# Experts stage: a store and a broadcast change places on SyncE, three steps move one unit, and an fp32 bias product becomes one fp16 product

## The chip, the cores and the metric

The kernel runs on one core of a Trainium2 chip. The metric is the device time of one execution in microseconds, as the median of several runs.

## The reference

The input is 4096 tokens of 128 channels (8 batches of 512, or 4 of 1024, as the layers see them). Six residual steps follow one another, each on a normalised copy of x:

```python
x = x + 0.5 * L0_ffn(layernorm(x))     # gate, up, down with a hidden width of 384
x = x + L0_attn(layernorm(x))          # time mixing with a scan over the tokens
x = x + 0.5 * L0_ffn(layernorm(x))
x = x + 0.5 * L1_ffn(layernorm(x))     # experts
x = x + L1_attn(layernorm(x))          # flow attention, causal
x = x + 0.5 * L1_ffn(layernorm(x))     # experts, the same weights
```

The change touches the experts step, cut to what matters:

```python
xn = (x - mu) * rsqrt(var + EPS) * ln_gamma + ln_beta
abel_out = gelu(xn @ abel_w + abel_b)
logits = xn @ moe_gate_w + moe_gate_b                        # 8 experts
topw, topi = top_k(logits, 2)
w_dense = sum(one_hot(topi, 8) * softmax(topw)[..., None])   # 8 weights a token, 2 of them not 0
h = gelu(einsum('bsd,edh->ebsh', xn, ew1) + eb1)             # 8 experts of width 256
eo = einsum('ebsh,ehd->ebsd', h, ew2) + eb2                  # eb2: the bias of the second layer, [8, 128]
moe_out = einsum('ebsd,bse->bsd', eo, w_dense)               # so eb2 comes in as w_dense @ eb2
moe_out = moe_out @ expm(gens[0]) @ expm(gens[1]) @ expm(gens[2])
gate = sigmoid(concatenate([abel_out, moe_out]) @ gc_w + gc_b)
mixed = abel_out * (1 - gate) + moe_out * gate
return residual + mixed
```

## The kernel before

x stays in SBUF for the whole program (`X`). Each of the six steps is a stage, and each stage runs over 8 chunks of 512 tokens. The stages and the order of every engine's work are written out by hand: each engine has a function per stage with a `step(i, p, lead, mid, lag)` that is called once per chunk. `mid` is the work on chunk i, `lead` prepares chunk i+1, `lag` finishes chunk i-1; the first call has only `lead`, the last only `lag`. Engines meet at semaphores. An instruction waits until its semaphore's count is reached, and everything behind it on its engine waits with it.

In the experts stages (numbers 4 and 6) the `mid` work on a chunk has 16 units u, two halves of 128 rows of each expert. Matrix products with fp32 accuracy are made of three fp16 products, high by high, high by low and low by high (`three`, lines 1474 to 1478). For each unit:

- TensorE makes the first layer's product into one of five PSUM banks (three products, 128x512),
- ScalarE takes the gelu in the bank (line 993),
- VectorE multiplies with the token's weight for that expert, giving `hw` (line 1317); the weights must lie in all 128 partitions, in `mo.wB`,
- ScalarE copies `hw` to fp16 (`high`, line 989), one unit behind its gelu,
- GpSimd subtracts that copy from `hw` and keeps the rest as fp16 (`low`, line 786),
- TensorE adds the second layer's product (`second`, line 1643) into bank 5, six units later (SKEW); units 10 to 15 of it fall into the next chunk's units 0 to 3.

The second layer's weights have the three rotations and a factor WS = 64 folded in, and so has the bias: `ebw` holds the folded bias in its first 8 rows and zeros below, and one fp32 product of `ebw` with `mo.wT` opens the sum in bank 5 (line 1641, just before unit 0 of `second`). `mo.wT` holds the 8 weights of each token in its first 8 rows, zeros below (written by the memset of line 741).

Between these units lies the routing of chunk i+1 (`lead`): TensorE turns the normalised tokens (line 1559, unit 1), ScalarE copies them to fp32 and fp16 (lines 999 and 1000, unit 2), TensorE makes the logits (line 1670, unit 3), VectorE finds the two largest and their weights in short dependent steps (lines 1349 to 1371, units 4, 6 and 7), TensorE turns the result to 8 rows (line 1682, unit 9), and VectorE copies that into `mo.wT` (line 1382, unit 9). The bank of the logits and of the turned weights is also that of the abel product (unit 11), which therefore waits for the copy. The finishing of chunk i-1 (`lag`) is on VectorE lines 1310 (unit 3), 1323 (unit 5), 1341 and 1344 (unit 10) and 1203 (unit 13), on ScalarE the tanh of line 1005 (unit 9), on TensorE lines 1665 and 1677 (units 8 and 12). ScalarE also normalises chunk i+2, one tile each in units 10, 11, 12 and 15 (line 903).

SyncE carries the weights to all partitions: `routes(c)` waits for `mo.wT`, writes its 8 rows to DRAM (line 613), waits for that, and issues four broadcasts of two experts each (line 617). In the second experts stage it also stores the finished chunks: for each c it first does `routes` of the next chunk, then waits for x of chunk c and stores it (line 627). x of chunk c is finished in unit 13 of the step of chunk c+1 (line 1203); the weights of chunk c+2 are ready in unit 9 of that same step.

## Time and profile before

| | us |
|---|---|
| timed runs, median (lowest to highest of 3) | 1024.81 (1024.4 to 1026.99) |
| the profiled execution | 1027.39 |
| its span, first to last instruction | 1025.7 |
| TensorE busy | 859.0 (84%) |
| VectorE busy | 725.1 (71%) |
| ScalarE busy | 648.1 (63%) |
| GpSimd busy | 604.2 (59%) |
| first experts stage, from its first transposes to its last x (about) | 307 to 543 |
| second experts stage (about) | 775 to 1023 |

Times in the trace are microseconds from the start of the span. PE is TensorE, PEld its weight loads, DVE VectorE, ACT ScalarE, POOL GpSimd, SPq the DMA queue of SyncE. L1317 is line 1317 of the kernel. Behind an instruction, brackets give how long its engine had been idle and which instruction ended the wait. The busy time of TensorE counts a product to its modelled end; one product of 128x512 is 0.38 long, and the next starts earlier.

### The profile page before, as it was taken

What the parts mean: (1) busy time and instruction counts of PE and PEld (TensorE: products, weight loads), DVE (VectorE), ACT (ScalarE), POOL (GpSimd) and SP (SyncE); (2) the same over time, 40 slices, a digit from 0 to 9 for tenths busy, and PEclk for the clock granted to TensorE, in tenths of its full rate; (3) what the DMA queues carried; (4) which work ended last, traced back from release to release, by engine and by line L of the source; (5) the groups of instructions that cost most, each with busy time, mean ns of one, the idle gap of its engine ahead of it and who ended that gap; (6) DMA issues with size and microseconds to landing.
All of it is one profiled execution on the core that took longest, in us unless ns stands there. A gap on an engine that the chain in (4) does not pass through costs nothing.

```text
span 1025.7 us, 14084 instructions
## 1 busy us (share of the span) xinstructions
PE 859.0 (84%) x3830; PEld 459.1 (45%) x3830; DVE 725.1 (71%) x1549; ACT 648.1 (63%) x1169; POOL 604.2 (59%) x611
## 2 busy tenths in 40 slices
PE   7889777678966999999994888888866998889997
PEld 6744333373423444444442455555534444444443
DVE  6945479964555788888872477777784878877774
ACT  3177499957745888888763343333324878777874
POOL 2164776566468776666673354444457757555664
PEclk9989799969986999999997899999986999999999
DMA  8000000000002222222200000000002221122220
GB/s 209 11 2 0 0 1 1 0 1 2 0 0 83 83 84 83 82 83 82 82 1 1 0 1 1 1 1 1 1 0 83 84 73 46 68 93 93 93 93 21
DMA packets 27406, 42.10 MB, mean 41 GB/s; under 512 B 5320, under 2 KB 19036, under 8 KB 27356
## 3 DMA queue, kind: packets, MB, share of 16 engines
q1 hardware_dynamic: 27356, 41.52, 12.2%
q8 instruction: 21, 0.34, 0.2%
q14 instruction: 29, 0.24, 0.1%
HBM read 39.15 MB, written 2.36 MB: 40 GB/s over the span
## 4 chain that ended last, share of the span: by engine, by line
PE 28%; issue 26%; POOL 21%; DVE 16%; ACT 5%; DMA 1%; SPq 1%; POOLq 1%; DVEq 0%; ACTq 0%
POOL arena L786 10%; PE bank L1476 5%; PE bank L1478 5%; PE bank L1477 5%; POOL arena L806 5%; POOL arena L750 4%; PE bank L1700 3%; DVE arena L1317 1%; ACT bank L993 1%; DVE stats L1166 1%; PE bank L1670 1%; PE bank L1707 1%; PE bank L1559 1%; DMA arena<-wrows 1%; ACT arena L989 1%
## 5 line engine op out<-in xcount | busy, mean ns | idle before, releaser
L786 POOL TENSOR_TENSOR arena<-arena 128x512 f16<-128x512 f32 x256 | 294.5, 1162 | 141.7 <-ACT arena L989 139.9
L1317 DVE TENSOR_TENSOR arena<-bank,arena 128x512 f32<-128x512 f32 x256 | 173.6, 685 | 89.7 <-ACT bank L993 48.5
L989 ACT ACTIVATE arena<-arena 128x512 f16<-128x512 f32 x256 | 161.3, 630 | 81.5 <-DVE arena L1317 81.0
L993 ACT ACTIVATE bank<-bank,eb 128x512 f32<-128x512 f32 x256 | 167.1, 657 | 18.1 <-PE bank L1478 17.2
L1477 PE MATMUL bank<-arena,ew1hi 128*128 128x512 f16 x256 | 101.6, 397 | 0.0
L813 POOL TENSOR_TENSOR arena<-arena 128x512 f32<-128x512 f32 (+1 forms) x24 | 32.7, 1372 | 117.0 <-DVE arena L1440 89.8
L1476 PE MATMUL bank<-arena,ew1hi 128*128 128x512 f16 x256 | 101.2, 395 | 0.0
L1478 PE MATMUL bank<-arena,ew1lo 128*128 128x512 f16 x256 | 101.1, 395 | 0.0
L1476 PE MATMUL bank<-arena,ew2hi 128*128 128x512 f16 x256 | 97.1, 379 | 0.8 <-POOL arena L786 0.6
L1477 PE MATMUL bank<-arena,ew2hi 128*128 128x512 f16 x256 | 97.0, 379 | 0.0
L1478 PE MATMUL bank<-arena,ew2lo 128*128 128x512 f16 x256 | 97.0, 379 | 0.0
L750 POOL TENSOR_TENSOR arena<-arena 128x512 f16<-128x512 f32 x48 | 54.8, 1157 | 58.0 <-ACT arena L917 58.0
L1707 PE MATMUL bank<-arena,until 128*128 128x512 f32 x128 | 63.2, 617 | 14.3 <-DVE arena L1396 13.1
L1476 PE MATMUL bank<-arena,f0hi 128*128 128x512 f16 x144 | 57.4, 399 | 16.7 <-POOL arena L750 13.5
L806 POOL TENSOR_TENSOR arena<-arena 128x1024 f32<-128x1024 f32 x32 | 61.7, 1949 | 0.0
L1407 DVE SCALAR_TENSOR_TENSOR arena<-arena,bank 128x1024 f32<-128x1024 f32 x16 | 19.5, 1222 | 54.4 <-PE bank L1700 54.4
L1477 PE MATMUL bank<-arena,f0hi 128*128 128x512 f16 x144 | 57.3, 398 | 0.0
L1478 PE MATMUL bank<-arena,f0lo 128*128 128x512 f16 x144 | 56.9, 395 | 0.0
L1227 DVE SCALAR_TENSOR_TENSOR arena<-bank,arena 128x512 f32<-128x512 f32 x48 | 33.0, 691 | 33.8 <-ACT arena L924 29.5
L903 ACT ACTIVATE Z<-X,nbias,rstd 128x128 f32<-128x128 f32 (+1 forms) x128 | 52.5, 487 | 5.4 <-POOL pool_spare L723 5.4
L1559 PE MATMUL bank<-ident,Z 128*128 128x128 f32 x192 | 31.9, 292 | 26.4 <-ACT Z L903 14.0
L1335 DVE TENSOR_SCALAR X<-X,keep,shift (+1 forms) x64 | 52.1, 818 | 0.0
(273 smaller groups left out, 1879.5 us busy)
## 6 DMA issues: line engine op xcount, KB each, us to landing
arena<-wrows SPq DMA_DIRECT2D x64, 512.0 KB, 5.6
X<-in_L_attn_x_dram SPq DMA_DIRECT2D x8, 256.0 KB, 4.3
out_dram<-X SPq DMA_DIRECT2D x8, 256.0 KB, 2.3
arena<-in_L_ffn_ew_dram SPq DMA_DIRECT2D x2, 512.0 KB, 6.5
arena<-in_L_ffn_ew_dram SPq DMA_DIRECT2D x1, 1024.0 KB
wrows<-arena SPq DMA_DIRECT2D x16, 16.0 KB
arena<-in_L_ffn_gens_dram SPq DMA_DIRECT2D x1, 192.0 KB, 2.6
arena<-in_L_ffn_w_gate_dram SPq DMA_DIRECT2D x1, 192.0 KB, 2.8
```

The lines of the kernel that those rows point to most:

```text
L750: pool.tensor_tensor(f0.hlo[:, u, :], f0.h[:, u % 2, :], f0.hhi[:, u, :], ALU.subtract).then_inc(S.hlo, 1)
L786: pool.tensor_tensor(mo.hlo[:, u % 8, :], mo.hw[:, u % 4, :], mo.hhi[:, u % 8, :], ALU.subtract).then_inc(S.hlo, 1)
L806: pool.tensor_tensor(fl.kv[:, b, :].rearrange("p (h m d) -> p h m d", d=HD, m=HD), key.to_broadcast([P, HEADS, HD, HD]), value.to_broadcas ...
L903: last = A(Z[:, zp, t * P:(t + 1) * P], X[:, bass.ds(tile * P, P)], ACT.Identity, bias=bias[:, bass.ds(tile, 1)], scale=scale[:, bass.ds(t ...
L989: A(mo.hhi[:, u % 8, :], mo.hw[:, u % 4, :], ACT.Copy).then_inc(S.hhi, 1)
L993: A(bank[MM1_BANK[u]][:, :], bank[MM1_BANK[u]][:, :], ACT.Gelu, scale=1.0 / WS, bias=eb1[:, u:u + 1]).then_inc(S.gelu, 1)
L1317: TT(mo.hw[:, u % 4, :], bank[MM1_BANK[u]][:, :], mo.wB[:, p, u // EB, :], ALU.mult)\
L1335: last = TS(tile, tile, keep[:, c], shift[:, c], ALU.mult, ALU.add)
L1476: mm(dst, whi, xhi, start=start, stop=False, skip_group_check=True)
L1477: mm(dst, whi, xlo, start=False, stop=False, skip_group_check=True)
L1478: return mm(dst, wlo, xhi, start=False, stop=stop, skip_group_check=True)
L1707: mm(bank[5 + h], until[:, :], fl.kv[:, b, h * CH:(h + 1) * CH], start=True, stop=True)\
```

## The change

Four edits, all in the experts stages or what prepares them:

1. SyncE stores chunk c-1 after the routing of chunk c+1 is sent, where it stored chunk c. The last store comes alone at the end.
2. The bias product becomes one fp16 product. `ebs` has the high part of the folded bias in rows 0 to 7 and 32 to 39 and its low part in rows 64 to 71; `mo.ws` has the high part of the weights in rows 0 to 7 and 64 to 71 and their low part in rows 32 to 39; all other rows are zero. ScalarE makes the two high parts of a chunk's weights from `mo.wT` in unit 15 of the chunk before (ahead of its last tile of normalising), VectorE the low part in unit 1 of the chunk itself, between line 1317 of units 0 and 1. The preparation of `ebs` takes three copies on ScalarE, where there was one, and a subtraction on VectorE in the third stage. The memset is of `mo.ws`, at the head of the third stage.
3. The turning of the routing weights and their copy move from unit 9 to unit 10, the abel product from unit 11 to unit 12.
4. In the first chunk of each experts stage ScalarE copies the next chunk's turned tokens after the gelu of unit 1, ahead of the fp16 copy of unit 0, where that was after unit 2's.

```diff
         ablo = sb("ablo", [P, P], F16)
-        ebw = sb("ebw", [P, P])
+        ebs = sb("ebs", [P, P], F16)
         gamma = sb("gamma", [P, 1])
...
         mo.wd = a.take([TILES, E])
-        a.used = max(a.used, TM_WORDS)
-        mo.wT = a.take([2, CH])
...
         fl.bdm = a.take([2, CH])
+        a.used = max(a.used, TM_WORDS)
+        mo.wT = a.take([2, CH])
+        mo.ws = a.take([2, CH], F16)
...
         MO.wd = sem("moe_wd")
+        MO.whi = sem("moe_whi")
+        MO.wlo = sem("moe_wlo")
         MO.wB = [sem(f"moe_wB{k}") for k in range(E // 2)]
...
         CREDIT = 1
+        Q = P // 4
...
             eng.wait_ge(FF.x, 2 * NCH + CREDIT)
-            eng.wait_ge(S0.flo, NU // TILES + 1)
+            eng.wait_ge(S0.flo, NU // TILES + 2)
             eng.wait_ge(S0.fhi, NU // TILES + 1)
...
+            def store(c):
+
+                sp.wait_ge(MO.x, c + (NCH + 1 + CREDIT))
+                sp.dma_start(out_parts[:, :, c:c + 1, :], X4[:, :, c:c + 1, :]).then_inc(stored, 16)
+
...
                     routes(NCH + c + 1)
-                sp.wait_ge(MO.x, c + (NCH + 1 + CREDIT))
-                sp.dma_start(out_parts[:, :, c:c + 1, :], X4[:, :, c:c + 1, :]).then_inc(stored, 16)
+                if c:
+                    store(c - 1)
+            store(NCH - 1)
             sp.wait_ge(stored, 16 * NCH)
...
                 pool.memset(blockones[:, :], 1.0).then_inc(S0.pool, 1)
-                pool.memset(ebw[:, :], 0.0).then_inc(S0.consts, 1)
+                pool.memset(ebs[:, :], 0.0).then_inc(S0.consts, 1)
                 pool.memset(ones[:, :], 1.0).then_inc(S0.consts, 1)
...
                     bias_parts()
-                    pool.memset(mo.wT, 0.0)
+                if number == 3:
+                    pool.wait_ge(S0.small2, 1)
+                    pool.memset(mo.ws, 0.0)
...
                 act.wait_ge(S0.consts, N_CONST)
-                A(ebw[0:E, :], bank[FOLD.small][0:E, P:2 * P], ACT.Copy, scale=WS).then_inc(S0.fhi, 1)
+                for row in (0, Q):
+                    A(ebs[row:row + E, :], bank[FOLD.small][0:E, P:2 * P], ACT.Copy, scale=WS)
+                A(sm.MT[0:E, :], bank[FOLD.small][0:E, P:2 * P], ACT.Copy, scale=WS).then_inc(S0.fhi, 1)
...
                         A(mo.hhi[:, u % 8, :], mo.hw[:, u % 4, :], ACT.Copy).then_inc(S.hhi, 1)
+                    def copies(i):
+                        act.wait_ge(S.tr, i + 2)
+                        A(mo.xn, bank[6][:, :], ACT.Copy).then_inc(S.xn, 1)
+                        A(mo.xhi[:, 1 - p, :], bank[6][:, :], ACT.Copy).then_inc(S.xhi, 1)
                     for u in range(NU):
...
                               bias=eb1[:, u:u + 1]).then_inc(S.gelu, 1)
+                            if u == 1 and not lag:
+                                copies(i)
                             if u:
                                 high(i, u - 1)
-                        if lead and u == 2:
-                            act.wait_ge(S.tr, i + 2)
-                            A(mo.xn, bank[6][:, :], ACT.Copy).then_inc(S.xn, 1)
-                            A(mo.xhi[:, 1 - p, :], bank[6][:, :], ACT.Copy).then_inc(S.xhi, 1)
+                        if lead and u == 2 and (lag or not mid):
+                            copies(i)
+                        if lead and u == NU - 1:
+                            act.wait_ge(S.wT, i + 2)
+                            for row in (0, 2 * Q):
+                                last = A(mo.ws[row:row + E, 1 - p, :], mo.wT[0:E, 1 - p, :], ACT.Copy)
+                            last.then_inc(S.whi, 1)
                         if onward and u in (10, 11, 12, 15):
...
                 TT(abel_b[:, :], abel_b[:, :], small[:, 2 * E + NU:2 * E + NU + 1], ALU.add).then_inc(S0.flo, 1)
+                dve.wait_ge(S0.fhi, NU // TILES + 1)
+                TT(ebs[2 * Q:2 * Q + E, :], sm.MT[0:E, :], ebs[0:E, :], ALU.subtract).then_inc(S0.flo, 1)
...
                     for u in range(NU):
+                        if mid and u == 1:
+                            dve.wait_ge(S.whi, i + 1)
+                            TT(mo.ws[Q:Q + E, p, :], mo.wT[0:E, p, :], mo.ws[0:E, p, :], ALU.subtract)\
+                                .then_inc(S.wlo, 1)
                         if lag and u == 3:
...
                                 add_to_x(i - 1, first, bank[6][:, :], 0.5, S.x, number)
-                        if lead and u == 9:
+                        if lead and u == 10:
                             dve.wait_ge(S.wpT, i + 2)
...
                             after(pe, S.dm, c)
-                            mm(bank[5][:, :], ebw[:, :], mo.wT[:, cp, :], start=True, stop=False,
+                            pe.wait_ge(S.wlo, c + 1)
+                            mm(bank[5][:, :], ebs[:, :], mo.ws[:, cp, :], start=True, stop=False,
                                skip_group_check=True)
...
                             pe.wait_ge(S.xn, i + 2)
+                            if mid:
+                                pe.wait_ge(S.wT, i + 1)
                             after(pe, S.abel, i)
...
                             last.then_inc(S.rT, 1)
-                        if lead and u == 9:
+                        if lead and u == 10:
                             pe.wait_ge(S.wpair, i + 2)
...
                             last.then_inc(S.wpT, 1)
-                        if mid and u == 11:
+                        if mid and u == 12:
                             if lead:
...
                             three(bank[7][:, :], abhi[:, :], ablo[:, :], mo.xhi[:, p, :], mo.xlo[:, p, :])\
```

## Rows read from the trace of the kernel before

**Rows 1.** busy by stretch: us, then PE, PEld, DVE, ACT, POOL; granted clock; DMA share, GB/s

```profile
433.20:460.40 27.20, 25.54 (x125) 12.50 (x125) 22.79 (x54) 22.68 (x44) 18.64 (x17) 1.00 0.22 78
876.70:907.10 30.40, 27.29 (x123) 12.94 (x123) 22.88 (x50) 22.42 (x43) 18.39 (x17) 0.94 0.24 78
```

**Rows 2.** timeline of TensorE (start us, us, instruction), the logits' products

```profile
351.80 0.95 PE L1670 MATMUL bank<-gate_g,arena 128*128 128x8 f32 x8
...
487.44 0.95 PE L1670 MATMUL bank<-gate_g,arena 128*128 128x8 f32 x8
...
818.08 0.95 PE L1670 MATMUL bank<-gate_g,arena 128*128 128x8 f32 x8
...
966.23 1.06 PE L1670 MATMUL bank<-gate_g,arena 128*128 128x8 f32 x8 [1.76 <-ACT arena L999]
```

**Rows 3.** timeline of TensorE, one middle chunk of the first experts stage

```profile
435.99 1.02 PE L1641 MATMUL bank<-arena,ebw 128*128 128x512 f32 x2
436.85 0.38 PE L1476 MATMUL bank<-arena,ew2hi 128*128 128x512 f16 x1
437.07 0.38 PE L1477 MATMUL bank<-arena,ew2hi 128*128 128x512 f16 x1
...
444.17 0.60 PE L1682 MATMUL bank<-ident,arena 128*8 128x128 f32 x4 [1.66 <-DVE arena L1371]
```

**Rows 4.** timeline of ScalarE, the same chunk

```profile
432.27 0.59 ACT L999 ACTIVATE arena<-bank 128x512 f32<-128x512 f32 x1
...
446.02 0.66 ACT L993 ACTIVATE bank<-bank,eb 128x512 f32<-128x512 f32 x1
...
454.56 0.63 ACT L989 ACTIVATE arena<-arena 128x512 f16<-128x512 f32 x1
```

**Rows 5.** timeline, the copy and the logits: first stage, then second

```profile
433.03 1.08 PEld L1670 LDWEIGHTS bank<-gate_g,arena 128*128 128x128 f32 x8
...
846.84 0.59 ACT L999 ACTIVATE arena<-bank 128x512 f32<-128x512 f32 x1
...
847.48 1.06 PE L1670 MATMUL bank<-gate_g,arena 128*128 128x8 f32 x8 [2.10 <-ACT arena L999]
```

**Rows 6.** waits of the second stage; timeline of SyncE's queue and VectorE

```profile
DVE arena L1317 <- DMA arena<-wrows: 25.5, 6, 4.4
...
837.57 0.39 SPq L627 DMA_DIRECT2D out_dram<-X  x1
...
840.03 1.81 SPq L617 DMA_DIRECT2D arena<-wrows  x4
...
844.41 1.29 DVE L1317 TENSOR_TENSOR arena<-bank,arena 128x512 f32<-128x512 f32 x2 [4.32 <-DMA arena<-wrows]
...
456.85 1.29 DVE L1317 TENSOR_TENSOR arena<-bank,arena 128x512 f32<-128x512 f32 x2 [1.47 <-ACT bank L993]
```

**Rows 7.** timeline of VectorE, the chunk of rows 3

```profile
446.29 0.67 DVE L1382 COPY arena<-bank 8x512 f32<-8x512 f32 x1
446.89 0.67 DVE L1317 TENSOR_TENSOR arena<-bank,arena 128x512 f32<-128x512 f32 x1
...
448.20 0.69 DVE L1344 SCALAR_TENSOR_TENSOR arena<-bank,arena 128x512 f32<-128x512 f32 x1
```

**Rows 8.** line 1364 (ns min/median/max), and GpSimd's timeline at the added subtraction

```profile
L1364 DVE TENSOR_TENSOR arena<-arena x16: 191/1030/1033, 313.1 to 974.7; 128x32 f32<-128x32 f32 x16
...
428.26 2.27 POOL L786 TENSOR_TENSOR arena<-arena 128x512 f16<-128x512 f32 x2 [0.84 <-ACT arena L989]
```

**Rows 9.** timeline, first chunk of the first stage, then of the second

```profile
325.74 5.61 POOL L786 TENSOR_TENSOR arena<-arena 128x512 f16<-128x512 f32 x5
...
328.28 0.69 DVE L1317 TENSOR_TENSOR arena<-bank,arena 128x512 f32<-128x512 f32 x1 [1.52 <-ACT bank L993]
...
790.39 1.88 PE L1670 MATMUL bank<-gate_g,arena 128*128 128x8 f32 x8 [4.01 <-ACT arena L999]
...
794.29 0.69 DVE L1317 TENSOR_TENSOR arena<-bank,arena 128x512 f32<-128x512 f32 x1 [1.59 <-ACT bank L993]
```

## The prediction, made before the changed kernel ran

> **What bounds the kernel now.** First the busy time by stretch [rows 1]: in a middle chunk of the first experts stage TensorE works 25.54 of 27.2 us at a granted clock of 1.00, ScalarE 22.68, VectorE 22.79. So TensorE leads, with little room behind it. Then the beat, from one chunk's gate logits (line 1670) to the next's [rows 2]. Five beats of the first experts stage take 487.44 - 351.80 = 135.64, 27.13 each. The same program in the second stage takes 966.23 - 818.08 = 148.15, 29.63 each. The question is what makes 27.13, and what adds 2.5 in the second stage.
>
> The timeline of one chunk answers the first. TensorE runs without a gap but for one: the transposes of the routing weights (line 1682) start at 444.17, after 1.66 us in which they wait for VectorE's line 1371 [rows 3]; with the 0.16 by which a product's modelled length (0.38) exceeds its step (0.22) the hole is 1.82. Then the chain on ScalarE: it copies the normalised input (line 999) at 432.27, and the logits' first weight load is at 433.03 [rows 4, 5]. Where TensorE did wait for that copy (846.84 to 847.48), it needed 0.64. So at 433.03 the copy had only 0.12 to spare; over the six like places I find 0 to 0.32 and take 0.18. ScalarE's chain (copy, logits, gelu, VectorE's routing chain, then gelus and fp16 copies without a gap to the next line 999) is thus 26.95 long against TensorE's 27.13: two loops of nearly one length. From the gelu at 446.02 to the copy at 454.56 ScalarE runs without a gap but the last 0.2: each operation starts some 0.52 after a copy of 0.63 and 0.57 after a gelu of 0.66 [rows 4].
>
> The waits answer the second [rows 6]: VectorE's line 1317 sat 25.5 us in six waits for the broadcast of the routing weights. SyncE issues the store of the previous chunk at 837.57 and the broadcasts only at 840.03; the first line 1317 that needs them starts at 844.41, after 4.32 of waiting. In the first stage, which stores nothing, the same instruction (456.85) waits 1.47, and for its gelu. SyncE held a finished routing row back for a store whose data came later. So the stall is 4.32 - 1.47, 2.85 a chunk, and ScalarE's loop there is 847.48 - 818.08 = 29.40 less 2.85, some 26.5 (shorter than in the first stage, for no statistics are taken there) [rows 2, 5].
>
> **The change part by part.**
>
> *SyncE.* The store of chunk c-1 now comes after the broadcasts of chunk c+1. All six stalls go: 2.85 each where ScalarE's loop is next. The weights are copied later (below), by 449.30 in the chunk of rows 3; even with the whole 2.46 from 837.57 to 840.03 after it, and the 4.38 from 840.03 to 844.41, line 1317 could start at 456.1, and it is wanted at 456.85 or later. The store now runs beside the last broadcasts, but their parts are used four or more units later.
>
> *TensorE's bias product.* fp32, 435.99 to 436.85, 0.86; as one fp16 product it is one step, 437.07 - 436.85 = 0.22 [rows 3]. It saves 0.64 a chunk, but ahead of the wait for line 1371, which VectorE and not TensorE sets: worth nothing in chunks with a successor, 0.64 in each last one.
>
> *Unit order.* The transposes move one unit on, behind six products (1.29). That fills 1.29 of the 1.82 hole. But VectorE's copy (line 1382), now in unit 10, stands behind hw, and in a middle chunk behind lines 1341 and 1344. It was at 446.29. hw of unit 10 can start when the gelu of 446.02 (0.66) is done, 446.71, so 0.18 before its 446.89; line 1344 then starts at 448.02, and the copy at 448.63 to 449.30 [rows 7]. TensorE, after its transposes (0.60 long, 0.44 by step) at 444.17 and four groups of three products, is at 447.2, waits for line 1344 to end (448.71), turns that result until 449.15, and waits for the copy until 449.36. With the abel product (three steps) behind it, unit 13's product comes at 450.01 instead of 449.58, so TensorE's loop is 27.13 + 0.43 = 27.56: the hole is not won but moved. The gelu of unit 13 lies in ScalarE's part without gaps, and TensorE is hardly ahead of it there: it starts some 0.42 later. ScalarE's loop takes that too, as does VectorE's, whose copy filled a slot that is now idle.
>
> *ScalarE's two added copies.* Of 8 x 512, at unit 15, in the part without gaps. No row shows such a copy on ScalarE. From below, nothing, if they fell into waits; from above 2 x 0.63 with no overlap. VectorE's copy of 8 x 512 takes 0.67, as much as its 128 x 512 ones at 0.67 to 0.69 [rows 7], so width and not partitions counts there; I take the step of ScalarE's 128 x 512 copies, 2 x 0.52 = 1.04. The Trainium skill (ScalarE: Activation LUTs, What ACT_TABLE_LOAD costs) speaks against the change here: an ACTIVATE goes by its elements per lane, 186 ns + 0.833 ns each, neighbours overlapping by 93 ns, whatever the partitions. By that page two cost an estimated 1.04 as well; if they went by all elements, they would be worth some 0.2.
>
> *VectorE's added subtraction* (8 x 512, between hw of unit 0 and of unit 1): 0.60 by its step. The fp16 copy of unit 1 follows a gelu and a copy later, so 0.02 of it shows. Its danger is GpSimd: line 1364 takes 0.19 to 1.03 us for the same 32 elements a partition [rows 8], the long ones beside a GpSimd operation. Here GpSimd's pair of low parts (428.26 to 430.53) ends near its place (430.44); with the fp16 copy of unit 15 moved as much as the gelu of unit 0, by some 1.46, I have the last one end 0.1 before the subtraction starts. The Trainium skill (GPSIMD Engine Reference, Specifications) says that VectorE instructions with two SBUF inputs contend with GpSimd for the SBUF interface; the long rows agree, and it is a rival below.
>
> *First chunk.* The copies of line 999 go ahead of the fp16 copy that waits for the broadcast. In the second stage the logits waited 4.01 for them (790.39), and hw of unit 4 was at 794.29 [rows 9]. Now its gelu can go right after those of units 2 and 3, and hw comes at 791.75: 2.5 earlier. In the first stage hw of unit 4 must wait until GpSimd has done its first low part, one of five from 325.74 (5.61, 1.12 each): 326.9 against 328.28, 1.4. At the end of these chunks the added copies take 1.04 back, less where ScalarE had been waiting (TensorE, not ScalarE, was late there); net 1.6 and 2.0 gained.
>
> *Rest.* The memset moves to the start of the third stage, GpSimd idle there before its first low part, under 1 us: nothing. Two more small copies at the end of mixing, at most 2 x 0.52: 0.3. One small subtraction in the third stage: nothing. New waits (whi, wlo, wT before the logits) find their work done half a chunk ago.
>
> *Sum.* First experts stage: beat 26.95 + 1.04 + 0.42 = 28.4, against 27.13 that is +1.2 to +1.3, five times +6.1; start -1.6; last chunk +0.43 - 0.64 = -0.2. Together +4.3. Second: beat 26.5 + 1.04 + 0.42 + 0.1 = 28.06, five of them 140.3 against 148.15, -7.8; start -2.0; into the last chunk and through it -1.6 (its stall is partly behind TensorE, 1.2; +0.43; -0.64; the rest of the tail 0.2). Together -11.4. With +0.3: -6.8. The profiled execution took 1027.39 (span 1025.7), so 1020.6; that one lies 2.6 above the median of the timed runs, 1024.81, from which it is 1018.0.
>
> **The rivals.**
> A. ScalarE's copies hide, and TensorE's loop of 27.56 binds. For it: ScalarE is busy only 22.68 of 27.2 [rows 1]. Against: its idle time is before units 5 to 7, in waits for VectorE, not at unit 15. Then the first stage gains 4.0 against my sum and the second 2.5: -13.3, 1011.5.
> B. The other sign: VectorE's subtraction is held by a GpSimd low part in each chunk. Place: between hw of units 0 and 1; price: up to 1.03 - 0.19 = 0.84 and what is left of the GpSimd operation (1.14), say 1.1 a beat, on ScalarE's loop, 12 beats, +13: 1031. It decides from 0.6 a beat on. For it, [rows 8]; against, the order of times above, and that only what exceeds 0.1 shows.
> C. TensorE's clock. The stretch at 876.70 has 0.94 of the full clock (products at the lower of the two levels, 1.2 GHz, after a pause before the logits) and is 30.40 long [rows 1]; the beat from 818.08, with such a pause and no fall, was 29.40. So 1.0 for each fall. My pauses (1.2 at line 1682, under 1 before the logits) are shorter than the present 1.82, which brings no fall. Seven of twelve beats would take the gain, twelve give 1030.
> D. The change doesn't do what it says: the broadcasts stay last, since the copy that feeds them moved back. Then the second stage keeps 29.6 a beat: 1018.0 + 7.8 = 1025.8.
>
> **How the numbers follow.** Forecast 0.60, A 0.20, B 0.08, C 0.06, D 0.06. What a measurement of this kernel can tell from no change is about 0.3%, 3.1 us. The forecast (its own range 1014 to 1022: copies 0.8 to 1.26, slack 0 to 0.32, copy's delay 0.2 to 0.6, each ten times) is faster nearly always, A always; B slower; C and D are the same or slower. Faster 0.79, same 0.12, slower 0.09. The range reaches into A below and near C above: 1010 to 1024.5.
>
> **What would show it.** In the trace after: no wait of line 1317 for the broadcast but the first of each stage; in both stages a beat of 28.1 to 28.4, the second stage gaining 1.5 a beat and the first losing 1.2; line 1682's hole shorter, a new one before the abel product; TensorE waiting for line 999 in every middle chunk, 0.5 to 0.9; two added copies of 0.6 each on ScalarE. The forecast is wrong if the first stage's beat stays at 27.1 to 27.6 (A), if the added subtraction is over 1.2 long (B), if clocks under 0.97 stand in middle chunks (C), or if waits for the broadcast remain (D).

## The result and the profile after

| | before | after |
|---|---|---|
| timed runs, median (lowest to highest, 13 each) | 1027.14 (1024.4 to 1030.39) | 1032.29 (1030.23 to 1034.93) |
| the profiled execution, its span | 1027.39, 1025.7 | 1031.05, 1029.3 |
| TensorE, VectorE, ScalarE, GpSimd busy | 859.0, 725.1, 648.1, 604.2 | 850.2, 735.4, 668.1, 606.8 |

The change makes the kernel slower by 0.50% (ratio 1.0050, 95% interval 1.0036 to 1.0065), some 5 us. The forecast was 1018.0. Of the 14.3 us between the two, 2.3 are the starting point: the forecast was counted from 1024.81, the median of three runs, where thirteen have 1027.14. As a difference, -6.8 was forecast and +5.1 measured. One of the executions behind the tables below (of "the same with the units of before") took 1276.51 us at a granted clock of 0.64, the four others of that version 1019.37 to 1021.56; it is left out.

The copy of the normalised input (line 999 before, line 1006 after) starts once a chunk and cuts the span into pieces. Timeline of ScalarE in the kernel before, the third and the eighth (last) such copy of each experts stage:

```profile
350.71 0.59 ACT L999 ACTIVATE arena<-bank 128x512 f32<-128x512 f32 x1
...
486.41 0.58 ACT L999 ACTIVATE arena<-bank 128x512 f32<-128x512 f32 x1
...
817.08 0.59 ACT L999 ACTIVATE arena<-bank 128x512 f32<-128x512 f32 x1
...
965.59 0.59 ACT L999 ACTIVATE arena<-bank 128x512 f32<-128x512 f32 x1
```

The same of the kernel after:

```profile
352.15 0.58 ACT L1006 ACTIVATE arena<-bank 128x512 f32<-128x512 f32 x1
...
497.08 0.58 ACT L1006 ACTIVATE arena<-bank 128x512 f32<-128x512 f32 x1
...
827.07 0.58 ACT L1006 ACTIVATE arena<-bank 128x512 f32<-128x512 f32 x1
...
970.14 0.58 ACT L1006 ACTIVATE arena<-bank 128x512 f32<-128x512 f32 x1
```

Five beats of the first stage take 144.93 after 135.70 (28.99 each, 27.14 before); of the second 143.07 after 148.51 (28.61 each, 29.70 before). With the first copy of each stage as a further cut, every kernel of this study falls into seven pieces. "First" is from the first to the third copy (the start of the pipeline and the step of chunk 0, in which the second copy lies), "seam" from the last copy of the first experts stage to the first of the second (the flow attention stage lies in it), "end" from the last copy to the end of the span:

| kernel | start | first | 5 beats | seam | first | 5 beats | end | span |
|---|---|---|---|---|---|---|---|---|
| before | 308.4 | 42.3 | 135.7 | 289.1 | 41.6 | 148.5 | 60.1 | 1025.7 |
| after | 308.6 | 43.6 | 144.9 | 288.6 | 41.4 | 143.1 | 59.2 | 1029.3 |
| forecast of after, against before | +0.3 | -1.6 | +6.1 | -0.2 | -2.0 | -7.8 | -1.6 | -6.8 |
| measured, against before | +0.2 | +1.3 | +9.2 | -0.5 | -0.2 | -5.4 | -0.9 | +3.6 |
| SyncE's order alone | 307.1 | 42.7 | 135.6 | 287.9 | 42.8 | 135.4 | 59.2 | 1010.7 |
| SyncE, units, first chunk | 310.7 | 41.6 | 137.4 | 291.2 | 39.1 | 137.4 | 60.7 | 1018.1 |
| bias product alone | 308.7 | 44.8 | 142.9 | 290.3 | 43.8 | 152.6 | 61.3 | 1044.4 |
| later units alone | 306.7 | 42.7 | 137.4 | 292.9 | 41.6 | 148.5 | 60.5 | 1030.3 |
| SyncE and first chunk | 308.6 | 41.5 | 135.6 | 289.1 | 42.0 | 135.4 | 59.2 | 1011.4 |
| subtraction late | 309.2 | 42.8 | 143.1 | 296.4 | 40.5 | 141.4 | 59.6 | 1033.0 |
| all late | 308.7 | 41.8 | 139.2 | 297.0 | 39.4 | 138.3 | 62.0 | 1026.4 |
| all late, old units | 309.1 | 41.7 | 136.6 | 291.8 | 42.4 | 136.4 | 60.9 | 1018.9 |
| subtraction in unit 9 | 308.4 | 43.3 | 153.0 | 292.9 | 41.2 | 151.2 | 64.8 | 1054.7 |
| third copy | 309.6 | 44.3 | 147.0 | 291.1 | 41.7 | 146.3 | 59.8 | 1039.7 |
| after, again | 308.8 | 43.3 | 144.1 | 290.5 | 41.0 | 143.1 | 59.1 | 1029.9 |
| all late, again | 309.2 | 41.8 | 138.3 | 296.7 | 39.2 | 138.3 | 62.0 | 1025.5 |

Of the 10.4 us by which the span missed its forecast (+3.6 against -6.8), 3.1 and 2.4 lie in the beats, 2.9 and 1.8 in the first chunks, 0.2 in the rest. Each row is one execution, and single pieces differ by chance: the starts lie between 306.7 and 310.7, though nothing that takes time in them was changed between most of these kernels.

The middle chunk of the kernel after, busy time by stretch (columns as in [rows 1]), once in each stage, against [rows 1]:

```profile
439.61:468.21 28.60, 25.68 (x122) 11.90 (x122) 22.88 (x56) 23.77 (x45) 18.70 (x16) 1.00 0.23 74
884.38:913.05 28.67, 25.66 (x122) 11.87 (x122) 22.78 (x52) 23.75 (x45) 18.70 (x16) 1.00 0.27 83
```

TensorE is no longer the engine with no room: 25.7 of 28.6 us against 25.54 of 27.2, at full clock, and it waits. The first of these stretches is the shortest of its stage's five; the others are 29.24, 29.22, 29.00 and 28.87, and VectorE is busy 0.8 to 0.9 longer in each. The same chunk in this execution and in the second one of the same kernel (the last experiment):

```profile
381.39:410.61 29.22, 25.80 (x122) 11.88 (x122) 23.79 (x57) 23.86 (x46) 18.53 (x16) 1.00 0.23 74
```

```profile
380.99:409.92 28.93, 25.80 (x122) 11.89 (x122) 22.94 (x57) 23.86 (x45) 18.71 (x16) 1.00 0.20 75
```

The difference is one instruction, line 1364, in which VectorE finishes a normalised tile of x. Timeline of VectorE and of GpSimd in the kernel after, a long and a short case:

```profile
428.80 1.26 DVE L1364 TENSOR_SCALAR X<-X,keep,shift  x1
...
457.81 0.33 DVE L1364 TENSOR_SCALAR X<-X,keep,shift  x1
```

```profile
428.76 1.22 POOL L798 TENSOR_TENSOR arena<-arena 128x512 f16<-128x512 f32 x1 [0.73 <-ACT arena L1003]
...
457.76 1.39 POOL L798 TENSOR_TENSOR arena<-arena 128x512 f16<-128x512 f32 x1 [0.72 <-ACT arena L1003]
```

Both start 0.04 to 0.05 after a GpSimd subtraction, and either outcome occurs. It was long in four of the five beats here and in one of five in the second execution. Compared chunk by chunk, a beat of the first stage is 0.28 to 0.29 longer with the long case, whichever execution has it; without it the five beats would average 28.76. In the second stage the last beat takes 28.50 with it and 28.51 without.

Timeline of TensorE in the chunk from 439.61, the instructions ahead of which it had been idle, and the bias product:

```profile
440.24 1.06 PE L1702 MATMUL bank<-gate_g,arena 128*128 128x8 f32 x8 [0.73 <-ACT arena L1006]
...
443.10 0.38 PE L1671 MATMUL bank<-arena,ebs 128*128 128x512 f16 x1
...
447.19 1.13 PE L1695 MATMUL bank<-arena,ones 128*128 128x512 f32 x2 [0.47 <-DVE arena L1352]
...
451.28 0.60 PE L1714 MATMUL bank<-ident,arena 128*8 128x128 f32 x4 [0.37 <-DVE arena L1400]
...
455.89 0.66 PE L1709 MATMUL bank<-ident,arena 128*128 128x128 f32 x4 [1.43 <-DVE arena L1373]
```

The first row is the verdict on who binds: the logits wait 0.73 for ScalarE, where in the first experts stage before the copy still had 0.12 to spare (433.03 in [rows 5]). The fourth and fifth are the moved hole: 0.37 where [rows 3] had 1.66, and 1.43 at a new place. ScalarE around unit 15 and around the next copy, the same kernel:

```profile
461.93 0.64 ACT L1003 ACTIVATE arena<-arena 128x512 f16<-128x512 f32 x1
462.47 1.25 ACT L1022 ACTIVATE arena<-arena 8x512 f16<-8x512 f32 x2
463.75 0.49 ACT L917 ACTIVATE Z<-X,nbias,rr 128x128 f32 x1
```

```profile
438.18 0.64 ACT L1011 ACTIVATE bank<-bank,eb 128x512 f32<-128x512 f32 x1
439.08 0.63 ACT L1003 ACTIVATE arena<-arena 128x512 f16<-128x512 f32 x1 [0.26 <-DVE arena L1346]
439.61 0.58 ACT L1006 ACTIVATE arena<-bank 128x512 f32<-128x512 f32 x1
440.09 0.59 ACT L1007 ACTIVATE arena<-bank 128x512 f16<-128x512 f32 x1
```

VectorE at the second of these places:

```profile
436.84 0.69 DVE L1346 TENSOR_TENSOR arena<-bank,arena 128x512 f32<-128x512 f32 x1 [2.76 <-ACT bank L1011]
437.56 0.68 DVE L1333 TENSOR_TENSOR arena<-arena 8x512 f16<-8x512 f32 x1
438.27 1.36 DVE L1346 TENSOR_TENSOR arena<-bank,arena 128x512 f32<-128x512 f32 x2
```

The two added copies take 462.47 to 463.75, 1.28, in a part of ScalarE's work without gaps. The subtraction takes 437.56 to 438.27, and hw behind it comes so late that the fp16 copy of 439.08 waits for it, a wait that [rows 4] do not have at their like place (432.27 follows its forerunners without one). From the gelu of 438.18 to the copy of the input at 439.61 are 1.43; in the kernel before the same two starts (431.18 and 432.27) are 1.09 apart. The difference, 0.34, is the subtraction's price on ScalarE's loop. The broadcasts are early, as meant. Waits of VectorE over the whole kernel after (columns: us, times, longest), where the second stage alone had 25.5 us in six waits [rows 6], and SyncE's queue in its second stage:

```profile
DVE arena L1346 <- DMA arena<-wrows: 4.9, 1, 4.9
```

```profile
872.56 0.28 SPq L617 DMA_DIRECT2D wrows<-arena  x1
...
874.04 1.74 SPq L621 DMA_DIRECT2D arena<-wrows  x4
...
876.11 0.39 SPq L627 DMA_DIRECT2D out_dram<-X  x1
```

The one wait left is that of the first chunk of the first stage; the store (line 627) stands behind the broadcasts.

### The profile page after: what moved, and what is told of

Read it like the earlier page. It is cut to its first block, busy times and chain, and to the rows that moved or that the text cites. A ratio compares the mean times of both kernels' runs of the same rounds, so it can differ in the third digit from the quotient of the medians.

```text
span 1029.3 us, 14102 instructions
## 1 busy us (share of the span) xinstructions
PE 850.2 (83%) x3805; PEld 447.3 (43%) x3814; DVE 735.4 (71%) x1566; ACT 668.1 (65%) x1203; POOL 606.8 (59%) x611
## 4 chain that ended last, share of the span: by engine, by line
POOL 30%; issue 23%; PE 21%; DVE 16%; ACT 8%; POOLq 1%; SPq 1%; DVEq 0%; DMA 0%; ACTq 0%
POOL arena L798 22%; PE bank L1732 9%; POOL arena L762 4%; PE bank L1739 3%; DVE arena L1436 2%; POOL rstd L720 1%; DVE arena L1346 1%; ACT bank L1011 1%; PE bank L1505 1%; DVE stats L1191 1%; PE bank L1507 1%; DVE arena L1438 1%; PE bank L1506 1%; ACT L1073 1%; ACT arena L1063 1%
## 5 line engine op out<-in xcount | busy, mean ns | idle before, releaser
L1346 DVE TENSOR_TENSOR arena<-bank,arena 128x512 f32<-128x512 f32 x256 | 174.1, 686 | 90.3 <-ACT bank L1011 76.6
L1505 PE MATMUL bank<-arena,ew1hi 128*128 128x512 f16 x256 | 98.3, 384 | 1.2 <-DVE arena L1346 1.2
L1506 PE MATMUL bank<-arena,ew1hi 128*128 128x512 f16 x256 | 98.3, 384 | 0.0
L1507 PE MATMUL bank<-arena,ew1lo 128*128 128x512 f16 x256 | 98.1, 383 | 0.0
L1425 DVE TENSOR_TENSOR arena<-bank,arena 128x512 f32<-128x512 f32 x64 | 42.4, 686 | 11.0 <-PE bank L1739 10.9
```

Of the source, the lines that this page charges most:

```text
L1346: TT(mo.hw[:, u % 4, :], bank[MM1_BANK[u]][:, :], mo.wB[:, p, u // EB, :], ALU.mult)\
L1505: mm(dst, whi, xhi, start=start, stop=False, skip_group_check=True)
L1506: mm(dst, whi, xlo, start=False, stop=False, skip_group_check=True)
L1507: return mm(dst, wlo, xhi, start=False, stop=stop, skip_group_check=True)
```

## The experiments

Times are against the kernel before in runs of the same chip, in three groups with medians of 1027.99 (the first four experiments), 1027.40 (the next four) and 1029.10 (the last four: subtraction in unit 9, third copy and the two repeats). A difference in us is the ratio times that median, unless another is named. The profiled executions of the bias product alone and of the moved subtraction were the slowest runs of these two versions, 3.9 and 2.8 above their medians, so their pieces add up to more than the timed difference. Theory: SyncE's order is worth its full gain; the loss is what the bias product lays on ScalarE's loop (1.28 of copies, 0.34 of subtraction), with the later units' 0.4 on top. The rivals: the later units carry it, or the broadcasts' gain was never there.

**SyncE's order alone.**

```diff
-                    routes(NCH + c + 1)
-                sp.wait_ge(MO.x, ...); sp.dma_start(out_parts ... c ...)
+                    routes(NCH + c + 1)
+                if c:
+                    store(c - 1)
+            store(NCH - 1)
```

> The kernel before with SyncE's new order alone: the store of chunk c-1 after the broadcasts of chunk c+1. Theory 1 (this part gives what the prediction gave it, and the loss is all in the other parts): the beats of the second experts stage fall from 29.63 to about 27.1 (five times 2.5 = 12.5), and the last chunk gives 1.2: -13.5 us; the first stage stays at 27.13 a beat. Theory 2 (TensorE or the clock takes most of it, as soon as the stall is gone): -5 to -8, beats of 28 to 28.6. Theory 3 (the order is worth nothing alone, since the broadcasts would stay last): 0.

Measured 1013.13, ratio 0.9866 (0.9834 to 0.9898), -13.8. Beats of 27.12 and 27.08. Theory 1. Busy time by stretch of this kernel:

```profile
431.29:458.20 26.91, 25.25 (x124) 12.38 (x122) 22.78 (x55) 22.41 (x44) 18.40 (x17) 1.00 0.23 79
870.20:897.33 27.13, 25.47 (x125) 12.47 (x124) 22.72 (x50) 22.32 (x43) 18.39 (x17) 1.00 0.23 88
```

Both stages now have the same beat at full clock: what the six stalls had added is gone. The rest of the change therefore costs 19 us (1032.29 - 1027.14 and 13.8).

**The change without its bias product.** (SyncE's order, the diff's units 10 and 12, the copies of the first chunk ahead; `ebw` and the fp32 product as before.)

```diff
-                            pe.wait_ge(S.wlo, c + 1)
-                            mm(bank[5][:, :], ebs[:, :], mo.ws[:, cp, :], start=True, ...
+                            mm(bank[5][:, :], ebw[:, :], mo.wT[:, cp, :], start=True, ...
```

> The change without its fp16 bias product (the fp32 product and its weights as before; no added copy on ScalarE, no added subtraction on VectorE): SyncE's order, the later units and the earlier copies of the first chunk. Theory 1 (the bias product's copies and subtraction carry the loss of 1.5 to 1.8 a beat): beats of about 27.5 in both stages, -13 us (-13.5 for SyncE, +0.4 a beat for the units, -2 to -3 for the two first chunks). Theory 2 (the later units or the first chunk carry the loss): beats of 28.3 and more, -5 to +3.

Measured 1018.30, ratio 0.9899 (0.9868 to 0.993), -10.4: theory 1 by its beats (27.48 and 27.47). Against SyncE's order alone the ten beats cost 3.7 and the first chunks give 1.1 and 3.7, but the seam is 3.3 longer and the end 1.5. (The start, 3.6 longer, has the same code in both: chance.)

**The bias product alone.** (The diff's `ebs`, `ws`, two copies, subtraction and product; SyncE, units and first chunk as before.)

```diff
+                        if lead and u == NU - 1:
+                            act.wait_ge(S.wT, i + 2)
+                            for row in (0, 2 * Q):
+                                last = A(mo.ws[row:row + E, 1 - p, :], mo.wT[0:E, 1 - p, :], ACT.Copy)
+                        if mid and u == 1:
+                            dve.wait_ge(S.whi, i + 1)
+                            TT(mo.ws[Q:Q + E, p, :], mo.wT[0:E, p, :], mo.ws[0:E, p, :], ALU.subtract)
```

> The kernel before with the fp16 bias product alone (two copies on ScalarE, one subtraction on VectorE, one product; SyncE, units and first chunk as before). Theory 1 (the added 1.28 of ScalarE and 0.34 of VectorE lie on ScalarE's loop): first stage's beat 28.5 to 28.7 against 27.13, +7 to +8 there; in the second stage the stall for the broadcast hides part, +0.3 to +1.0 a beat; +9 to +12 us in all. Theory 2 (the copies hide and the later units carry the loss): 27.2 to 27.6 a beat in the first stage, 0 to +2.

Measured 1042.24, ratio 1.0131 (1.0098 to 1.0165), +13.5. The first stage's beat is 28.57, as theory 1 has it: 26.95 + 1.28 + 0.34 = 28.57. The second stage's beat, 30.53, is 0.83 above that of the kernel before, inside its range. The whole time is above its own (+9 to +12), for the first chunks are 2.5 and 2.2 longer, which the expectation did not have. What the second stage's beat is made of, the windows say:

```profile
411.00:439.53 28.53, 25.48 (x122) 12.03 (x122) 23.60 (x57) 23.73 (x45) 18.46 (x16) 1.00 0.20 74
...
830.45:860.07 29.62, 25.33 (x122) 11.99 (x122) 23.48 (x52) 23.61 (x45) 18.45 (x16) 1.00 0.23 72
...
890.93:921.57 30.64, 28.41 (x122) 13.30 (x122) 23.63 (x52) 23.84 (x45) 18.50 (x16) 0.89 0.22 76
```

Where the clock is granted in full the beat is 29.62; with the stall for the broadcast and ScalarE's late copy both in it, the clock falls (0.89: part of the stretch at the lower level), and the beats are a further 1.0 to 1.3 longer. That is my rival C, in a kernel where the stalls are still there; in the whole change no middle chunk shows it.

**The later units alone.**

```diff
-                        if lead and u == 9:      # VectorE's copy, TensorE's turn
+                        if lead and u == 10:
-                        if mid and u == 11:      # abel
+                        if mid and u == 12:
```

> The kernel before with the later units alone (weights' turn one unit on for VectorE, TensorE's transposes and the abel product). Theory 1 (as predicted: TensorE's hole is moved, not won, +0.43 a beat in the first stage; hidden in the second by the stall for the broadcast): first stage's beat 27.56, +2 to +3 us. Theory 2 (the units carry the loss, since the later copy of the weights comes too late for all that follows): a beat of 28.3 or more in the first stage, +6 or more. Theory 3 (the hole is won): 26.95 to 27.0 a beat, -1.

Measured 1033.89, ratio 1.0059 (1.0028 to 1.009), +6.1. (TensorE also waits for the weights' copy ahead of the logits, as in the change.) The first stage's beat is 27.47, +0.33: theory 1's mechanism, not theory 2's. Those beats sum to 1.7 us. Of the 4.6 by which its span is longer, 3.8 lie in the seam, which theory 1 did not have: right by the beats, the time is twice its range.

**SyncE's order and the first chunk, no later units, no bias product.**

```diff
+                            if u == 1 and not lag:
+                                copies(i)
-                        if lead and u == 2:
+                        if lead and u == 2 and (lag or not mid):
```

> The kernel before with SyncE's order and the earlier copies in the two first chunks (and TensorE's wait for the weights' copy ahead of the logits), without the later units and without the fp16 bias product. Theory 1 (the first chunks' gain of 1.2 in the first stage and some 2.5 to 3.5 in the second was real, and eaten by the bias product's copies): beats of 27.1, and first chunks shorter by 1.2 and 2.5, so -16 to -18 us. Theory 2 (the earlier copies gain only beside the later units, or what they give is lost at the next wait): -13 to -15.

Measured 1013.75, ratio 0.9867 (0.9839 to 0.9895), -13.7: theory 2 by the time. First chunks 1.2 and 0.8 shorter than with SyncE's order alone, not 1.2 and 2.5, and the seam 1.2 longer. The second stage's first chunk by stretch, in SyncE's order alone, in this kernel, and in the one without the bias product:

```profile
773.28:816.09 42.81, 34.34 (x140) 17.53 (x141) 27.30 (x78) 29.52 (x55) 30.16 (x40) 0.76 0.30 100
```

```profile
774.85:816.82 41.97, 33.37 (x140) 15.71 (x141) 28.30 (x82) 29.06 (x54) 30.49 (x40) 0.84 0.30 102
```

```profile
780.88:820.02 39.14, 31.58 (x145) 15.28 (x145) 27.88 (x82) 28.81 (x54) 30.49 (x40) 0.91 0.30 109
```

The granted clock differs (0.76, 0.84, 0.91), and the length goes with it: these chunks begin at the lower level and come out of it at different moments. How much of the 3.7 was the earlier copies and how much the clock, these profiles don't tell.

**Only the subtraction moved.** (To unit 0 of the next step; the bias product to unit 13 of the second layer, where it needs it last.)

```diff
-                        if mid and u == 1:
-                            dve.wait_ge(S.whi, i + 1)
+                        if lag and u == 0:
+                            dve.wait_ge(S.whi, i)
```

> The whole change with ScalarE's copies where they are (unit 15), only VectorE's subtraction moved to unit 0 of the next step ahead of hw, and the bias product into unit 13 of the second layer. Theory 1 (0.34 of the subtraction and 1.28 of the copies add up on ScalarE's loop): beats shorter than those of the whole change by 0.3 to 0.4, some 28.65 and 28.25, and about +1 to +2 us against the kernel before. Theory 2 (the subtraction delays nothing that matters, the whole loss is the copies'): beats as in the whole change (28.99 and 28.61), +5.

Measured 1031.93, ratio 1.0038 (1.0018 to 1.0057), +3.9. Beats 28.62 and 28.27, 0.37 and 0.34 less than in the whole change: the subtraction's share, as computed. (The second figure is the cleaner: in the first stage line 1364 was long in all five beats here, in four there.) The whole time is worse than expected for another reason (seam, below).

**Everything moved.** (The copies, besides, to ScalarE's wait before the fp16 copy of unit 7.)

```diff
-                        if lead and u == NU - 1:
-                            act.wait_ge(S.wT, i + 2)
+                            if u == 8:
+                                act.wait_ge(S.wT, i + 1)
```

> The whole change, but its added work moved to idle places: ScalarE's two copies into its wait before the fp16 copy of unit 7 of the chunk itself, VectorE's subtraction to unit 0 of the next step ahead of hw, the bias product into unit 13 of the second layer. Theory 1 (the loss is the place of 1.28 on ScalarE and 0.34 on VectorE, both in ScalarE's loop): beats of 27.4 to 27.6 in both stages, as without the product, and -10 to -12 us against the kernel before. Theory 2 (there is no idle place left, what is added there delays VectorE's routing chain or the units behind it): beats of 28 and more, -5 to +3.

Measured 1027.94, ratio 1.0001 (0.9982 to 1.002), and again, below, 0.9982. Beats 27.84 and 27.65: between the theories, nearer to the first. Timeline of this kernel: ScalarE's copies, then VectorE's subtraction, then the GpSimd operation beside it:

```profile
443.86 1.25 ACT L1018 ACTIVATE arena<-arena 8x512 f16<-8x512 f32 x2
445.84 0.63 ACT L1003 ACTIVATE arena<-arena 128x512 f16<-128x512 f32 x1 [0.73 <-DVE arena L1346]
```

```profile
457.89 1.56 DVE L1333 TENSOR_TENSOR arena<-arena 8x512 f16<-8x512 f32 x1
...
459.48 1.29 DVE L1346 TENSOR_TENSOR arena<-bank,arena 128x512 f32<-128x512 f32 x2
```

```profile
457.74 1.16 POOL L798 TENSOR_TENSOR arena<-arena 128x512 f16<-128x512 f32 x1 [0.73 <-ACT arena L1003]
```

The copies cost nothing there: the fp16 copy behind them still waits 0.73 (1.91 in the version without the product, 1.2 more). The subtraction is 1.56 long, twice its 0.68.

And the seam is 8.4 longer than in the whole change. In the step that only finishes the last chunk, the subtraction stands behind VectorE's variances for the next stage, and TensorE waits for it in the middle of its last products:

```profile
541.58 0.59 PE L1672 MATMUL bank<-arena,ebs 128*128 128x512 f16 x1 [3.35 <-DVE arena L1333]
```

That is a fault of my placement, not of the change.

**The same with the units of before** (9, 9 and 11).

> As the one before (copies, subtraction and bias product at idle places), and the units as in the kernel before (turn and copy of the weights at unit 9, abel at 11). Theory 1 (the later units cost 0.35 to 0.4 a beat, all else hides): beats of 27.1, -15 us. Theory 2 (the later units matter only together with the copies at unit 15, or the added copies at unit 8 cost something now): beats of 27.4 and more, -10 to -12.

Measured 1020.26, ratio 0.9925 (0.99 to 0.995), -7.7. Beats 27.33 and 27.28, 0.5 and 0.4 less than with the later units, but 0.2 above the 27.1 of theory 1; the time lies between that theory's and its rival's. SyncE's order alone remains better.

**Subtraction in unit 9.**

```diff
-                        if lag and u == 0:
+                        if mid and u == 9:
```

> As the version with the late copies (units of the change), but VectorE's subtraction right after them, in unit 9 of the chunk itself, where VectorE waits for the gelu. In the late version its subtraction at unit 0 was 1.56 long at 457.89 instead of 0.68. Theory 1 (a GpSimd operation lay beside it, and only that keeps the late version at 27.84 a beat): a subtraction of 0.6 to 0.7, beats of 27.5, and some 3 to 4 us less than the late version. Theory 2 (the late bias product itself or the copies at unit 8 cost the 0.36): beats of 27.8 again. If the subtraction is long here too, VectorE's routing units are later and the beat is 28.

Measured 1059.19, ratio 1.0307 (1.0267 to 1.0347). The last sentence of the expectation, and worse: 30.6 a beat. Timeline of VectorE, then TensorE's row that follows from it, then a stretch:

```profile
426.44 1.56 DVE L1333 TENSOR_TENSOR arena<-arena 8x512 f16<-8x512 f32 x1
```

```profile
430.71 0.66 PE L1710 MATMUL bank<-ident,arena 128*128 128x128 f32 x4 [2.69 <-DVE arena L1373]
```

```profile
412.39:443.15 30.76, 27.00 (x124) 12.50 (x123) 25.27 (x56) 24.07 (x45) 18.39 (x16) 0.94 0.21 69
```

Beside GpSimd's work (425.18 to 427.45) the subtraction is long once more; it now delays line 1373, the hole before TensorE's transposes grows from 1.43 to 2.69, and the clock falls to 0.94. One 8-row subtraction, placed where VectorE looked idle, costs 2.8 us a beat (30.6 against 27.84) over the version that has it at unit 0. In the second stage the first beat still has the full clock and takes 28.68 (27.20 there); the others, at 0.94, take 30.40 to 30.75 (27.7 to 27.8 there). So about 1.5 of it is the later work, and the rest comes with the clock.

**A third copy.**

```diff
-                            for row in (0, 2 * Q):
+                            for row in (0, 2 * Q, 3 * Q):
```

> The whole change with a third copy of 8 x 512 on ScalarE at unit 15 (into rows that the product multiplies by zero). Theory 1 (what lies on ScalarE at unit 15 is paid in full in each beat, 0.64 a copy): beats of 29.6 and 29.25 against 28.99 and 28.61, +7 to +8 us against the whole change. Theory 2 (the beat's loss is mostly elsewhere, a copy costs less than its step): +0 to +4.

Measured 1041.29, ratio 1.0128 (1.0086 to 1.017), +9.2 us over the whole change in the same group (1032.05). Beats 29.39 and 29.26. In the second stage that is +0.65. In the first it is +0.40 against the 28.99 of the whole change, but line 1364 was short in all five beats here; against the 28.76 that the whole change has without its long cases it is +0.63. Paid in full in both. The three take 1.92, 0.64 each. Theory 1.

**The whole change and the late version again.**

> The whole change once more, for its seam between the first experts stage and the second (from the last copy of the normalised input in the one to the first in the other, 288.60 us; 289.09 in the kernel before, 292.93 with the later units alone). Theory 1 (the length of the seam belongs to the program, through the moment at which TensorE's clock falls after the last chunk): 288 to 289.5 again, with the same granted clocks from 50 us after that copy on. Theory 2 (it is chance, other in every execution): anything from 287 to 297. Beats 28.99 and 28.61 in both.

> The late version once more, for its seam of 297.04 us, 8.4 longer than in the whole change. Theory 1 (it belongs to the program): 296 to 298 again, and the same clocks. Theory 2 (chance): anything from 287 to 297, and times then that spread as far.

Measured 1032.05, ratio 1.0052 (1.0034 to 1.007), beats 28.81 and 28.62, seam 290.53; and 1027.49, ratio 0.9982 (0.9958 to 1.0006), beats 27.66 and 27.66, seam 296.72. The first stage's beat of the whole change is 0.18 shorter than in the first execution: three fewer long cases of line 1364. The late version's long seam belongs to it: 297.04 and 296.72, and 296.4 with only the subtraction late. Its wait of 3.35 is not the whole of it, for the late version with the units of before has the same wait and a seam of 291.8; its stretch of 60 us that begins 48 us after the last copy has a granted clock of 0.83, the late version's 0.72. Why the clock falls further there is not shown. The shorter differences do not belong to a program: the whole change had 288.60 and 290.53. In the whole change that stretch had 0.83 in the one execution and 0.80 in the other:

```profile
545.08:605.08 60.00, 38.83 (x126) 21.88 (x129) 24.96 (x42) 19.80 (x34) 25.16 (x27) 0.83 0.00 0
```

```profile
544.10:604.10 60.00, 38.73 (x115) 20.68 (x118) 22.46 (x40) 18.51 (x32) 25.18 (x27) 0.80 0.00 0
```

So of a single profiled seam, 2 us are chance; what the later units cost there (3.8 in one profile, 3.3 in another) is not settled; the whole change has them too, with a seam no longer than before.

## Why the prediction was wrong

The mechanism held (ScalarE's loop binds, the stall for the broadcast goes, the hole moves); what failed are two terms of ScalarE's loop and the first chunks. The beats miss by 5.5 us, the first chunks by 4.7. None of the four signs of being wrong came, for the beats went above the forecast 28.1 to 28.4 and no sign was given for that side.

- **SyncE: right.** Six stalls gone, -13.8 alone, where the 12.5 of five beats and 1.2 more had been reckoned before it ran. D is refuted.
- **Unit order: right in kind, its size of 0.42 hit by luck.** The hole is moved (0.37 and 1.43; of the forecast wait for the copy behind it the trace shows none). With the product, beats are 28.99 with the later units and 28.57 without, 0.42; but chunk by chunk it is 0.17 to 0.20 where line 1364 is short and 0.46 to 0.49 where it is long, and it was long in four of five. The 3 to 4 us that single profiles show in the seam were not in the sum.
- **ScalarE's two copies: right mechanism, price too low.** 1.28, not 1.04. The step of 0.52 that I took from the 128x512 copies includes an overlap of 0.1 with what follows them [rows 4]; behind these two there is none, 0.64 each, and the third copy again 0.64. My upper bound of 2 x 0.63 was the value. The Trainium skill (ScalarE: Activation LUTs, What ACT_TABLE_LOAD costs) was followed in that the partitions don't count: 8 rows cost as much as 128, and here the trace agrees; its overlap of 93 ns between neighbours is not seen behind these copies, and the measurement decides.
- **VectorE's subtraction: the step that failed outright.** I had 0.02 a beat in the first stage and 0.1 in the second, since the fp16 copy of unit 1 comes "a gelu and a copy later". But hw of unit 1 was itself only just in time: pushed back by 0.71 it makes that copy wait 0.26, and ScalarE's copy of the input comes 0.34 later in all. Taking it away from there gave 0.37 and 0.34.
- With both, the first stage's beat is 26.95 + 1.28 + 0.34 = 28.57 (measured 28.57 in the bias product alone), with the 0.19 that the later units were found to add 28.76 (28.76 without the long cases of line 1364), and with their 0.23 on average 28.99 (28.99). The second's is 26.5 + 1.28 + 0.34 + 0.42 = 28.54 (28.61), its 26.5 and 0.42 being estimates that no run isolates. The two mispriced terms, 0.56 and 0.48 a beat, make 5.2 of the 5.5 us that the beats miss. (The recorded sum also has +6.1 where its own terms, 28.41 against 27.13, give +6.4.)
- **First chunks: forecast 1.6 and 2.0 shorter, measured 1.3 longer and 0.2 shorter.** This step failed too, for 4.7 us in all. The price of the bias product there was not 1.04, "less where ScalarE had been waiting": without the product they are 0.7 and 2.4 shorter than before (the second partly by its clock, 0.91 against 0.84), with it 2.0 and 2.3 longer than that, and alone in the kernel before it costs 2.5 and 2.2. The variants part it: moving the subtraction away takes 0.7 and 0.9 off (43.6 to 42.8, 41.4 to 40.5), moving the copies too another 1.0 and 1.1 (to 41.8 and 39.4), each from one profile. Timeline of TensorE, whole change:

```profile
348.15 0.66 PE L1588 MATMUL bank<-ident,Z 128*128 128x128 f32 x4 [0.99 <-ACT Z L917]
...
823.08 0.33 PE L1588 MATMUL bank<-ident,Z 128*128 128x128 f32 x1 [0.99 <-ACT Z L917]
```

  The last normalised tile of the next chunk (line 917) stands behind the added copies on ScalarE, and TensorE, which has no lead in these chunks, waits 0.99 for it. In the version without the product no such wait stands there. In the first stage 0.7 more is missing from my 1.4: hw of unit 4 came at 327.57, not 326.9, for the low part it waits for starts at 326.29, not at 325.74 [rows 9]; 0.38 of that is one operation of GpSimd's (line 721) that takes 0.58 instead of 0.20 beside the added subtraction of 322.22.
- **Rivals.** A fell (beats of 28.99). B did not happen in the change: all 16 subtractions take 0.68, since the next GpSimd operation starts at 438.35, 0.11 after the end at 438.24. But its price is real: moved beside one, the same instruction takes 1.53 to 1.56. And the same neighbourhood struck elsewhere, at line 1364: 0.93 longer in four beats of the profiled execution, some 1.2 us, which the prediction did not price. C happened only in variants (bias product alone, subtraction in unit 9). My 1030 to 1031 for B and C lie near the result for reasons that are not its own.

What the forecast did wrong as a whole: it saw that ScalarE's loop and TensorE's are equally long, and then took a step of 0.52 for copies whose durations it had at up to 0.63, and next to nothing for a subtraction ahead of a copy whose slack it had not measured. On a loop without slack such an omission is paid in every beat.

The best version here is SyncE's order alone, 1013.13, 1.3% faster than before and 1.8% faster than the whole change; the earlier copies add nothing to it that can be measured (1013.75, -13.7 against -13.8).

## What to carry over

Where two engines' loops are equally long, trading 0.64 us of one for 1.62 of the other loses; look for the loop behind the busiest engine before relieving it. Price an added instruction in a part without gaps by its whole duration, and follow the one queued behind it to the wait that it just met. Compare repeated executions chunk by chunk before a sum that fits to 0.01 is believed: here an instruction that came out long or short by chance was worth 0.23 of a beat. A change made of several parts should be timed in its parts: here one was worth 13.8 us and another cost 13.5.

## What the runs showed of the hardware

- Copies of 8x512 on ScalarE, one behind another: 0.64 a step each, in pairs and threes, and what follows them does not overlap them either (462.47 + 1.28 is the 463.75 of line 917); copies of 128x512 step 0.52 at a duration of 0.63 [rows 4]. It is not that two copies follow one another: lines 1006 and 1007, both 128x512 copies, start 0.48 apart at a duration of 0.58. What in the 8x512 copies makes the difference was not told apart.
- VectorE's 8x512 subtraction with both inputs in SBUF: 0.68 alone, 1.53 to 1.56 beside GpSimd's subtraction, though it touches 8 partitions. The Trainium skill (GPSIMD Engine Reference, Specifications) states contention for the shared SBUF interfaces with VectorE instructions that have two SBUF inputs; these rows agree.
- VectorE's line 1364, one tile of x scaled and shifted in place in SBUF, took 0.33 or 1.26 when it started 0.04 to 0.05 after a GpSimd subtraction; in the short case GpSimd's own took 1.39 instead of 1.22. Which of the two it was differed between executions of one program.
- Middle chunks kept the full clock with TensorE's pauses of 1.43, 0.73, 0.47 and 0.37 in them, and with the subtraction in unit 9 stood at 0.94 in nine of ten chunks with one of 2.69; the tenth, from 838.71, kept 1.00. In the bias product alone it was 0.94 and 0.89 in chunks that began with a pause of 2.15 and 2.21. The length of one pause does not settle it: in the kernel before, the chunk with 2.10 [rows 5] kept the full clock, and the one at 876.70 [rows 1], which began with 1.79, had 0.94.
